# Gated-feature attention: one round in another order, larger blocks cut in pieces, two block copies from ScalarE to VectorE, and the norm's last step from VectorE to GpSimd

## What is computed

```
Q = (x @ Wq.T + bq) in 4 heads of 64;  K, V = context in 4 heads
gen = head @ proj.T + proj_b           # 24 numbers: A(8), Bg(8), Th(8) clipped to +-8
psi = [A*exp(Th) + Bg*cos(Th),  Bg*sin(Th)]        # 16 features, for Q and for K
tensor = qr.kr + qi.ki ; spinor = qr.ki - qi.kr
wedge  = sqrt(max(|q|^2 |k|^2 - tensor^2 - spinor^2, 0) + 1e-6)
hodge  = sqrt(|q|^2 + 1e-6) * sqrt(|k|^2 + 1e-6)
scores = (g0*wedge + g1*tensor + g2*spinor + g3*hodge) / 4 / temperature
out = softmax(scores) @ V @ Wo.T + bo ;  x = layernorm(x + out)
```

## Time and profile before

| what | us |
|---|---|
| median of 3 runs (2824.83 to 2836.79) | 2835.43 |
| the profiled execution | 2834.78 |
| its span, first to last instruction | 2833.1 |
| `psi` scores begin / last residual of `psi` begins / first matmul of the next layer's product | 2058.0 / 2574.3 / 2592.9 |
| five full rounds (first Relu of round 1 to first Relu of round 6) | 326.78 |

### The profile page before, as it was taken

One profiled execution on the slowest core, in us unless ns is written; L12 is line 12 of the kernel. 1 busy time (PEld: TensorE's weight loads), 2 busy tenths in 40 slices (PEclk: granted clock), 3 DMA queues, 4 the chain that ended last, 5 costly groups with the idle time before them and its releaser, 6 DMA issues. The chain is left out here.

```text
span 2833.1 us, 32030 instructions
## 1 busy us (share of the span) xinstructions
PE 2371.9 (84%) x11624; PEld 1503.3 (53%) x11624; DVE 1695.8 (60%) x3500; ACT 1363.7 (48%) x1968; POOL 325.7 (11%) x299
## 2 busy tenths in 40 slices
PE   6888888876888888887999699997568878777998
PEld 4656666652333333334566456565355655555886
DVE  5666666624666666654643598989566666743232
ACT  2333333311555555562222565654188888782221
POOL 0000000000000000000156400000111111100000
PEclk7999999966999999999899899998789999998999
DMA  2000000006333333214034512111200000002000
GB/s 77 8 16 15 16 16 15 8 8 165 53 68 68 61 66 57 47 27 162 16 59 65 106 38 68 45 68 46 102 8 31 30 31 30 23 15 75 15 23 23
DMA packets 104949, 132.46 MB, mean 47 GB/s; under 512 B 21748, under 2 KB 87556, under 8 KB 104792
## 3 DMA queue, kind: packets, MB, share of 16 engines
q1 hardware_dynamic: 90440, 115.58, 15.2%
q0 software_dynamic: 11904, 14.69, 3.2%
q10 hardware_dynamic: 2448, 0.14, 0.1%
HBM read 73.69 MB, written 31.20 MB: 37 GB/s over the span
## 5 line engine op out<-in xcount | busy, mean ns | idle before, releaser
L987 DVE TENSOR_REDUCE xattn_tops<-region 128x2 f32<-128x1024 f32 x256 | 306.3, 1220 | 128.9 <-PE region L771 128.8
L924 ACT ACTIVATE xattn_probs<-region 128x1024 f32<-128x1024 f32 x256 | 256.3, 1022 | 126.1 <-PE region L760 125.0
L156 PE MATMUL region<-gla_xT,weights_even 128*128 128x512 f32 (+1 forms) x416 | 200.6, 637 | 21.0 <-ACT gla_xT L248 21.0
L760 PE MATMUL region<-xattn_qs,xattn_ks 49*128 49x512 f32 x512 | 126.6, 496 | 61.8 <-DVE xattn_tops L987 31.4
L156 PE MATMUL region<-mamba_xT,weights_odd 128*128 128x512 f32 x320 | 156.4, 636 | 3.1 <-DVE mamba_xh L1988 3.1
L2491 DVE CUSTOM_DVE_ANT_0 weights_even<-psi_wedge,region,psi_unsign 128x512 f32<-128x512 f32 x128 | 95.4, 746 | 98.9 <-ACT psi_wedge L2325 97.3
L156 PEld LDWEIGHTS region<-gla_xT,weights_even 128*128 128x128 f32 (+1 forms) x416 | 77.1, 192 | 133.9 <-issue 107.0
L789 PE MATMUL region<-xattn_probs,xattn_va 128*32 128x512 f32 x1024 | 142.6, 624 | 1.4 <-ACT xattn_o_T L951 1.4
L771 PE MATMUL region<-xattn_ks,xattn_qs 48*128 48x512 f32 x512 | 126.5, 493 | 13.0 <-DMA xattn_ks<-xattn_khi 8.6
L165 PE MATMUL region<-weights_even,gla_work 128*128 128x256 f32 x512 | 119.6, 394 | 17.6 <-DVE gla_work L631 11.0
L760 PEld LDWEIGHTS region<-xattn_qs,xattn_ks 49*128 49x128 f32 x512 | 48.9, 190 | 141.0 <-DVE xattn_tops L987 70.8
(11 more groups left out here) (534 smaller groups left out, 5377.4 us busy)
## 6 DMA issues: line engine op xcount, KB each, us to landing
weights_even<-mamba_cs SPq DMA_DIRECT2D x32, 512.0 KB, 4.7
xattn_qs<-xattn_qhi SPq DMA_DIRECT2D x128, 64.0 KB, 2.3
xattn_ks<-xattn_khi SPq DMA_DIRECT2D x128, 64.0 KB, 2.3
moe_sums<-moe_picked SPq DMA_DIRECT2D x9, 512.0 KB, 7.8
gla_x<-in_x SPq DMA_DIRECT2D x8, 512.0 KB, 3.8
x_after_gla<-gla_res SPq DMA_DIRECT2D x8, 512.0 KB, 2.9
xattn_x<-x_after_gla SPq DMA_DIRECT2D x8, 512.0 KB, 4.1
xattn_ctxT<-in_ctxT SPq DMA_DIRECT2D x8, 512.0 KB, 4.4
```

What stands on the lines that cost most here:

```text
L156: last = st.nc.tensor.matmul(o[0:m, i, :], w[:, c, col + i * P:col + i * P + m], rhs[:, c, :], start=c == 0, stop=c == kc - 1)
L760: last = mm(o[:, r, :], ks[rows, ring(n), a, j * P:j * P + P], qs[rows, ring(n), a, :], start=True, stop=True)
L924: A_(probs[:, p % 3, a, :, :], st.region(f"k{v}")[:], ACT.Exp).then_inc(st.emptying(f"k{v}"), 1)
L987: V.tensor_reduce(tops[:, n % 2, t, a::2], st.region(f"q{u}")[:], AX, ALU.max).then_inc(st.emptying(f"q{u}"), 1)
```

## The change

Three things are done in `psi_layer`. The order of a round is another one. Four steps are cut in pieces that stand apart in the order: Q in two halves, gen in two (the half that needs only the context first), pv in two per pair of heads, out in two, and the first split in two. And work changes engine: blocks 1 and 2 of fT are copied by DVE instead of ACT, and the norm's subtract-and-multiply is done by POOL instead of DVE. The reciprocal of the sums is now a step of its own (`recip`) at the head of the round.

```diff
             for b in range(-2, B + 1):
                 yield "score", b, 0
+                yield "recip", b - 1, 0
                 yield "features", b + 1, 0
...
                     elif what == "pv":
+                        c, part = divmod(i, 2)
...
-                        for j in range(NT):
+                        for j in (2 * part, 2 * part + 1):
...
-                    elif what == "fT":
+                    elif what == "fT" and i not in (1, 2):
                         act.wait_ge(*st.full(f"fT{b}_{i}"))
...
+                    elif what == "fT" and i in (1, 2):
+                        dve.wait_ge(*st.full(f"fT{b}_{i}"))
...
+                        o = st.region(f"fT{b}_{i}")
+                        if i == 1:
+                            V.tensor_copy(fL[0:64, 0, :], o[0:64, 0, :])
+                            V.tensor_copy(fL[64:P, 1, :], o[64:P, 0, :])
+                            last = V.tensor_copy(fQ[:, 0, :], o[:, 1, :])
+                        else:
+                            V.tensor_copy(fK[0:64, 0::2, :], o[0:64, :, :])
+                            last = V.tensor_copy(fK[64:P, 1::2, :], o[64:P, :, :])
...
                     elif what == "norm":
                         x = xs[b % XS]
                         dve.wait_ge(*st.emptied(f"out{b}"))
-                        norm.vector(dve, nth, x, x, "x_out")
+                        if b:
+                            dve.wait_ge(st.sem("x_out"), b)
+                        norm.moments(dve, nth, x)
...
                         norm.gpsimd(pool, nth, K["neg_half"], 1e-5)
+                        x = xs[b % XS]
+                        pool.wait_ge(st.sem("rstd0"), b + 1)
+                        for t in range(NT):
+                            last = G.tensor_scalar(x[:, t, :], x[:, t, :], norm.mv[:, t, 0:1], norm.rstd[:, t:t + 1],
+                                                   ALU.subtract, ALU.mult)
+                        last.then_inc(st.sem("x_out"), 1)
```

More of the change, by code:

```diff
@@ L2110, in order @@
                 yield "score", b, 13
+                yield "out", b - 1, 0
+                yield "split", b + 1, 1
                 yield "angles", b + 2, 1
                 yield "score", b, 14
+                yield "out", b - 1, 1
                 yield "angles", b + 2, 2
+                yield "split", b + 1, 2
                 yield "score", b, 15
@@ L2145, in _ @@
                     elif what == "Q":
[L2146 to L2149, removed]
-                    elif what == "gen":
[L2151 to L2161, removed]
+                        if i == 0:
+                            pe.wait_ge(*st.emptied(f"xT{b}"))
+                            if b == 0:
+                                weights.arrive(pe)
+                            st.claim(f"Q{b}")
@@ L2226, in _ @@
                     elif what == "out":
-                        for c in range(DC):
-                            pe.wait_ge(*st.emptied(f"pv{b}_{c}"))
-                        token_major(st, f"out{b}", featT, wo)
+                        if i == 0:
+                            for c in range(DC):
+                                pe.wait_ge(*st.emptied(f"pv{b}_{c}"))
+                            st.claim(f"out{b}")
+                        o = flat(st.region(f"out{b}")[:])
+                        for t in (2 * i, 2 * i + 1):
+                            for c in range(DC):
+                                last = mm(o[:, t * D:t * D + D], featT[:, c, t * P:t * P + P], wo[:, c, :],
+                                          start=c == 0, stop=c == DC - 1)
+                        if i:
+                            last.then_inc(st.filling(f"out{b}"), 1)
             @block.sync
@@ L2286, in _ @@
                         A_(featT[:], st.region(f"xT{b}")[:], ACT.Copy).then_inc(st.emptying(f"xT{b}"), 1)
-                    elif what == "Q":
+                    elif what == "Q" and i == DC - 1:
                         act.wait_ge(*st.full(f"Q{b}"))
@@ L2309, in _ @@
                             last = A_(fA[:, n, :, :], o[:], ACT.Copy)
-                        elif kind == "rest":
+                        else:
                             A_(fL[0:64, 2 * n, :], o[0:64, 0, :], ACT.Copy)
```

101 lines of the change are left out of this document (63 added, 38 removed).

## The result

The changed kernel takes 2903.48 us (median of 4 runs, 2897.58 to 2920.07), the kernel before 2832.85 (4 runs): ratio 1.0262, 95% interval 1.0213 to 1.0312. It is slower, on the side that had the larger chance, but 50 us above the forecast and 28 above the wider range of 2808 to 2875.

A forecast was written before the change was run, and what follows sets the result against it. ACT sets the time only in a round's third part, where DVE's later end would replace it. 2834.8 + 22.7 (five full rounds, +4.5 each) - 4.5 (the rest) = 2853 us; own range 2840 to 2866, wider range 2808 to 2875.

The forecast's parts named there:

- the first part: Full round from its first to its ninth Relu: 26.55 us against 24.56 before, +2.0.
- the lock: First part: features 3 on DVE slowed beside POOL's bias addition; at most 2.0 us, within 1.4 charged for both uncertain costs.
- the clock: First part: PE's granted clock falling after two idle stretches; at most 1.0 us, within 1.4 charged for both uncertain costs.
- the transposes of two blocks: Third part, after the residual: PE transposes two blocks while DVE stands; 2.1 us with hand-over.
- the second and third together: Full round from its ninth Relu to its end: 43.35 us against 40.24 before, +3.1.
- the casts: DVE's copies of blocks 1 and 2 out of PSUM: near 0.6 us half-size and 1.2 full-size.
- the turn's wait: First part: ACT waits 1.9 us before the first turn copy, for PE behind DVE's second score.
- The rest: Outside the five full rounds: round 0 -3.5, rounds 6 and 7 +2.5, after the last round a gain; together -4.5 us.
- The tail: After the last round: first pv under the exponentials -5, norm's step on POOL +1.2, hand-over 0.3.
- Rival 1: DVE's copies and PE's half blocks fit beside ACT, each of eight rounds gains 3.74: 2801 us; chance 0.18.
- Rival 2: Even: interleaving saves in the first part what the third loses, round 65.5, whole 2831 us; chance 0.20.
- Rival 3: DVE's copies wait for POOL's four steps, its chain growing 2.6 in each of seven rounds: 2871 us; chance 0.10.

The follow-up runs named there:

- e10: The changed kernel with extra, unread matmuls on PE at the round's head only, ahead of score 2 and turn 4; 2877.3 us, ratio 1.0164.
- e3: The changed kernel with extra, unread matmuls on PE in three places, before feature block 0, score 2 and the first ACT turn; 2866.66 us, ratio 1.0115.
- e17: The kernel before, order and undivided steps kept, with both engine moves (two block copies to DVE, norm's step to POOL); 2815.57 us, ratio 0.9962.
- e5: The changed kernel with the sums and the features' slice at the round's head back in their old places; 2878.09 us, ratio 1.0162.

## Why the prediction was wrong, step by step

**The step that failed** is in the first part: "For both I take 1.4, between 0 and 3.0 (2.0 for the lock, 1.0 for the clock)". The lock was sized within its bounds (2.93 less 1.09 is 1.8; with the clock kept up, in e10, 0.8). The clock was not: I took 1.0 as its most, because before one idle of 3.94 had gone with .86. e10 shows that the lost clock, with what it drags along, adds 6.3 us to that part in four of five rounds (32.6 against 26.3) and 1.3 in the other. And I charged nothing for it in the third part, though the prediction itself made PE wait there for the residual: e3 shows 1.7 per round (23.5 against 21.8). Nearly all of that is in the transposes of two blocks, from block 0's start to DVE's first cast: forecast 2.1, measured 3.68, and 1.98 in e3. Together 384.2 - 351.5 = 32.7 us over five rounds.

**The rest of the sum for a full round held.** With the clock kept up (e3) the first part is 26.3 to 27.3 us (26.55 forecast), the second and third together 43.5 (43.35), the five rounds 351.5 (349.5). DVE's last score came 3.45 us behind ACT's last Sqrt (3 forecast), so that ACT's 3.74 was not gained; the casts took 0.68 and 1.21 (0.6 and 1.15); the turn's wait was 2.81 (1.9), and 1.93 in e10. The forecast's own range was added up wrongly: its bounds on the uncertain costs and the copies give 2843 to 2870, not 2840 to 2866.

**"The rest" was the second wrong term.** Forecast -4.5, measured 1.7 + 7.4 + 3.4 - 1.0 = +11.5, 16 us off. For round 0 I counted only ACT's gain in the third part (2.2 came, of 3.5) and left the rest alone. Its second part became 1.7 shorter, but its first went from 18.15 to 23.78: ACT waits 1.52 us at score 3, and 3.54 at score 7 behind features 3, one instruction of which is held to 2.73 us beside POOL's bias addition (0.68 alone). For rounds 6 and 7 I estimated +2.5 and got +10.8; with PE filled (e3) they still took 66.0 and 41.2 against 60.7 and 36.4 before, so most of this is not won back with the clock and goes with the order. The tail gained 1.0 of the 3.5: POOL's step took 4.83 and not 2.6, within its bounds.

**Rivals.** Rival 1 (ACT stays the bound) is false in the new order by its own condition, and true in the old one: e17's third part. Rival 2 fell: even with the clock kept up the first part is 26.3 (e10) against 24.7 before, and with sums and features back in their places (e5) it is 2 us shorter. Rival 3 (POOL holds DVE) is nil, the casts beside L2593 being as long as elsewhere; the Trainium skill's rule (SBUF — State Buffer, section "Who interferes with whom") agrees with both rows, since features 3, with two inputs from SBUF, was held. A rule that I did not use would have warned: the Trainium skill (TensorE: Matmul & The Clock Gate, section "HAM oscillation — how this bites in real kernels") describes a kernel whose wait in every tile puts the clock back each time, and here the granted clock was .68 to .88 in the first part and .78 to .85 in the third, behind waits of 1.6 to 6.2 us in each of the five rounds.

## What to carry to other kernels

When a reordering gives TensorE new waits, price them twice: the wait, and the work behind it at the clock's lower level until the granted clock is seen to return; a part that showed 1.00 before has room to lose. Ask of each step that is moved what it was covering: moving the product with V off the head took away the work that filled TensorE there and lengthened the end of the round. And test engine moves apart from an order: here the moves gained 0.4 to 0.9% in the old order, each alone nothing, and the new order hid that in a loss of 2.6%.

## Not expected of the hardware

Useless matmuls made the kernel 37 us faster (e3), though they release nothing for another engine. POOL's subtract-and-multiply of 128x256 took 1.21 us each whatever ran beside it; the Trainium skill's rate for simple bodies (GPSIMD Engine Reference, section 3.1) gives near 1 us for all four, an estimate, so the measurement decides. The same first part, instruction for instruction, took 27.59 or 32.65 us in neighbouring rounds, with a granted clock of .88 and .74.
